# A recommendation model's interaction tower: chunk 0's shifted tiles picked by TensorE, earlier ids, products and norms, stacked context tiles

## Chip, cores and metric

The kernel runs on one core of one Trainium2 chip. The metric is the device time in microseconds of one execution. Lower is better.

## The reference

39 ids per example pick rows of 16 values from 39 tables (x, for 512 examples). Three layers then multiply fields pairwise and mix them with a weight matrix; each layer's result is divided by its norm per example, feeds the next layer, and its sum over the 16 values is a feature. Three dense layers end it.

```python
for k in range(3):
    z = jnp.einsum('bmd,bhd->bdmh', x, prev).reshape(b, D, m * h)
    t = jnp.einsum('bdc,co->bdo', z, ws[k]) + bs[k]
    t = jnp.transpose(t, (0, 2, 1))
    norm = jnp.sqrt(jnp.sum(t * t, axis=(-2, -1), keepdims=True))
    t = t / norm
    logit.append(t); prev = t
z = jnp.sum(jnp.concatenate(logit, axis=1), axis=-1)
h = jnp.concatenate([z, dense_ctx], axis=1)        # 384 + 16 features
h = jnp.maximum(h @ W_top1 + b_top1, 0.0)
h = jnp.maximum(h @ W_top2 + b_top2, 0.0)
y = h @ W_top3
```

## The kernel before

The batch is cut into 16 chunks of 32 examples. A chunk's x has 39 fields as rows and 512 columns (32 examples by 16 values).

**Gathering x.** SP loads the ids and the tables' first rows (L393, L394). POOL adds them (`make_rows`, L305) and issues ten indirect gathers for a chunk (`gather`, L320). SP stores the gathered rows to `x_scratch` in HBM (`store_chunk`, L386 to L390) and loads them back (`load_pairs`, L280, L286): three copies of x one above the other (`x_rep`, 3 x 39 rows) and, in `x_rot`, seven tiles in which the same rows stand shifted by 1, 2, ... fields. The tiles come in four groups, [0, 1], [2, 3], [4, 5], [6]; group 0's semaphore also counts x_rep. For chunk 0, ACT's queue loads groups 1 and 3.

**Layer 0.** DVE multiplies x_rep by each tile (`make_pairs`, L734), and PE sums the products with the folded w0 in seven float32 matmuls into `acc0` (`pair_matmul`, L619). `turn_x` (L607) transposes x for the scalars of the later layers.

**Layers 1 and 2.** Their products would be too many, so PE multiplies the previous result by all weights first, and ACT and DVE multiply by x afterwards. A float32 product is made of three f32r matmuls: the previous result and the weights are each split in a rounded part and the rest (`prev_hi`, `prev_lo`, `w_hi`, `w_lo`), and `three_terms` (L554 to L556) writes one PSUM bank of four fields by 128 units. A job is a layer, a chunk and a quarter of its columns; it has ten banks, D and A in turn (`PATTERN`). DVE takes the five D banks field by field (`add_field`, L756) and merges (`merge`, L775). ACT scales the five A banks (`scale_bank`, L441) and POOL adds them (`add_bank`, L333). A banks run LEAD = 7 ahead of the job that PE is in. After the merge PE turns the sum into `turned` (`turn_sums`, L595), one job later. There are 128 jobs: 0 to 3 are chunk 0 in layer 1, 4 to 7 chunk 1 in layer 1, 8 to 11 chunk 0 in layer 2, and so on in iterations of eight.

**The order around it** is written in tables of (job, place). `FINISHES` says at which A bank ACT adds the bias and squares (`finish`, L465, L468) and after which field DVE sums both (L779, L783). `NORMS` says where PE sums the squares over the units (`norms`, L632), ACT takes the root (L475), and DVE the reciprocal in four steps, the new prev (L821) and the features (L811). `HALVES_AT` says where ACT makes prev_hi (L481) and POOL prev_lo (`low`, L338). `PAIRS_AT` and `PAIR_MATMULS_AT` place the products and matmuls of layer 0 for the next chunk. Each engine works in order.

**The start.** ACT's queue loads w1, w0, the biases, w2; ACT rounds the weights (`split_high`, L424) and DVE subtracts (`split_low`, L723). PE runs `keep_busy` matmuls (L639) whose results aren't used.

**The end.** `top1` (L684) has four output tiles of four float32 matmuls: the 16 context rows (k = 0) and three features of 128 rows. Then top2 (L708) and top3 (L714).

## Time and profile before

| | us |
|---|---|
| median of 3 runs | 1101.58 (1101.01 to 1102.05) |
| the profiled execution, its own time | 1101.28 |
| its span, first to last instruction | 1099.6 |
| PE busy | 1052.5 (96%) |
| DVE busy | 969.0 (88%) |
| POOL busy | 866.9 (79%) |
| ACT busy | 780.5 (71%) |

The span is what the profiler saw between the first and the last instruction; the execution's time has 1.7 us around it. Busy shares are means over stages. The chain of waits goes back from the last instruction and says at each moment what the end hung on.

### The profile page before, as it was taken

The page shows a single profiled execution, that of the slowest core. Times are in us where ns is not written, and L with a number is a line of the kernel's source. Part 1 is how long each engine was busy: PE and PEld are TensorE (multiplying, and loading weights), DVE is VectorE, ACT ScalarE, POOL GpSimd, SP SyncE. Part 2 cuts the span into 40 slices and gives each one's busy share as a digit, 9 for nine tenths or more (in the row PEclk, how much of TensorE's full clock was granted, in tenths as well). Part 3 has the DMA queues.
Part 4 walks back from the last instruction along what each step waited for, and adds up shares of the span by engine and source line. Part 5 has one row for each costly group of instructions (what it writes and reads, how often), then busy time and mean ns, then how long its engine had stood idle before and what let it go on. Part 6 is the DMA issues. An engine that isn't in the chain of part 4 may idle for free.

```text
span 1099.6 us, 17904 instructions
## 1 busy us (share of the span) xinstructions
PE 1052.5 (96%) x4394; PEld 794.1 (72%) x4394; DVE 969.0 (88%) x3317; ACT 780.5 (71%) x2628; POOL 866.9 (79%) x726
## 2 busy tenths in 40 slices
PE   0798999999999999999999999999999999999999
PEld 0366687777778787777778777777777777788773
DVE  2467799998999999999999999999999999899892
ACT  3266586877768687776868777786868777688762
POOL 5587798888889888888888888888888888577660
PEclk9899999999999999999999999999999999999999
DMA  6503040110303011030303002030301203000000
GB/s 228 131 13 73 2 118 7 35 41 3 73 3 73 2 35 42 5 71 3 73 2 71 5 11 66 3 73 2 74 2 20 56 3 73 0 2 1 1 1 1
DMA packets 56735, 41.20 MB, mean 37 GB/s; under 512 B 37915, under 2 KB 40859, under 8 KB 56502
## 3 DMA queue, kind: packets, MB, share of 16 engines
q1 hardware_dynamic: 49145, 32.17, 12.5%
q10 hardware_dynamic: 2365, 6.60, 1.7%
q0 software_dynamic: 5120, 1.29, 1.3%
q8 instruction: 35, 0.57, 0.2%
q14 instruction: 70, 0.57, 0.2%
HBM read 38.09 MB, written 1.94 MB: 36 GB/s over the span
## 4 chain that ended last, share of the span: by engine, by line
PE 67%; POOL 21%; issue 6%; ACT 4%; DMA 1%; DVE 0%; SPq 0%; POOLq 0%; ACTq 0%
POOL sums L333 17%; PE bank_a L554 10%; PE bank_d L554 9%; PE acc L619 9%; PE bank_d L555 9%; PE bank_d L556 9%; PE bank_a L556 9%; PE bank_a L555 9%; POOL gathered L320 4%; ACT scaled L441 2%; PE turned L595 1%; ACT sums L441 1%; PE bank_a L684 1%; DMA x_pairs<-x_scratch 1%; PE bank_d L708 1%
## 5 line engine op out<-in xcount | busy, mean ns | idle before, releaser
L333 POOL TENSOR_TENSOR sums<-sums,scaled 128x512 f32<-128x512 f32 (+1 forms) x512 | 642.8, 1256 | 154.0 <-ACT scaled L441 119.3
L756 DVE SCALAR_TENSOR_TENSOR sums<-bank_d,x_col,sums 128x128 f32<-128x128 f32 x2304 | 654.8, 339 | 74.4 <-PE bank_d L556 58.8
L441 ACT ACTIVATE scaled<-bank_a,x_col 128x128 f32<-128x128 f32 x1920 | 550.6, 382 | 152.9 <-PE bank_a L556 144.4
L554 PE MATMUL bank_d<-w_hi,prev_lo 128*128 128x512 f32 x640 | 286.1, 447 | 1.2 <-DVE sums L775 0.9
L554 PE MATMUL bank_a<-w_hi,prev_lo 128*128 128x512 f32 (+1 forms) x640 | 274.5, 429 | 12.0 <-POOL prev_lo L338 6.3
L556 PE MATMUL bank_d<-w_hi,prev_hi 128*128 128x512 f32 x640 | 253.3, 396 | 0.0
L555 PE MATMUL bank_d<-w_lo,prev_hi 128*128 128x512 f32 x640 | 253.0, 395 | 0.0
L556 PE MATMUL bank_a<-w_hi,prev_hi 128*128 128x512 f32 (+1 forms) x640 | 246.2, 385 | 0.0
L555 PE MATMUL bank_a<-w_lo,prev_hi 128*128 128x512 f32 (+1 forms) x640 | 245.9, 384 | 0.0
L441 ACT ACTIVATE sums<-bank_a,x_col 128x128 f32<-128x128 f32 x512 | 146.1, 370 | 88.3 <-PE bank_a L556 88.3
L320 POOL DMA_INDIRECT gathered<-in_table,idx x160 | 177.2, 1107 | 31.9 <-issue 21.7
L554 PEld LDWEIGHTS bank_a<-w_hi,prev_lo 128*128 128x128 f32 x640 | 120.6, 188 | 66.0 <-issue 20.9
L554 PEld LDWEIGHTS bank_d<-w_hi,prev_lo 128*128 128x128 f32 x640 | 121.0, 189 | 42.0 <-DVE sums L756 8.7
L555 PEld LDWEIGHTS bank_a<-w_lo,prev_hi 128*128 128x128 f32 x640 | 121.1, 189 | 37.2 <-issue 13.7
L555 PEld LDWEIGHTS bank_d<-w_lo,prev_hi 128*128 128x128 f32 x640 | 121.7, 190 | 29.7 <-issue 10.8
L556 PEld LDWEIGHTS bank_d<-w_hi,prev_hi 128*128 128x128 f32 x640 | 121.0, 189 | 28.9
L556 PEld LDWEIGHTS bank_a<-w_hi,prev_hi 128*128 128x128 f32 x640 | 120.8, 189 | 22.7
L619 PE MATMUL acc<-z,w_sb 117*128 117x512 f32 (+1 forms) x224 | 115.9, 605 | 0.7 <-issue 0.7
L734 DVE TENSOR_TENSOR z<-x_pairs 117x1024 f32<-117x1024 f32 x64 | 106.8, 1672 | 5.1 <-DMA x_pairs<-x_scratch 4.9
L756 DVE SCALAR_TENSOR_TENSOR bank_d<-bank_d,x_col,sums 128x128 f32<-128x128 f32 x256 | 78.8, 348 | 0.0
L775 DVE TENSOR_TENSOR sums<-bank_d,sums 128x128 f32<-128x128 f32 x256 | 71.3, 279 | 0.4 <-DVE sums L756 0.4
L619 PEld LDWEIGHTS acc<-z,w_sb 117*128 117x128 f32 (+1 forms) x224 | 42.4, 195 | 15.0 <-issue 6.0
(59 smaller groups left out, 484.7 us busy)
## 6 DMA issues: line engine op xcount, KB each, us to landing
x_pairs<-x_scratch SPq DMA_DIRECT2D x141, 156.0 KB
x_pairs<-x_scratch SPq DMA_DIRECT2D x78, 78.0 KB
gathered<-in_table,idx POOLq DMA_INDIRECT x160
w_raw<-in_w ACTq DMA_DIRECT2D x2, 768.0 KB, 7.2
x_scratch<-gathered SPq DMA_DIRECT2D x16, 72.0 KB
w_raw<-in_w ACTq DMA_DIRECT2D x1, 1024.0 KB, 5.7
w_raw<-in_w ACTq DMA_DIRECT2D x1, 896.0 KB
w_raw<-in_w ACTq DMA_DIRECT2D x1, 832.0 KB
```

The lines of the kernel that those rows point to most:

```text
L320: nc.gpsimd.indirect_dma_start(out=gathered[0:n, c % 2, j, :], out_offset=None, in_=table[:, :], in_offset=bass.IndirectOffsetOnAxis(ap=id ...
L333: nc.gpsimd.tensor_tensor(out=sums[:, n % SUMS, 0:w, :], in0=sums[:, n % SUMS, 0:w, :], in1=scaled[:, a - 1, 0:w, :], op=ALU.add).then_inc ...
L441: op = nc.scalar.activation(to[:, i, :], bank_a[at % A_RING][:, i * UNITS:(i + 1) * UNITS], ACT.Copy, scale=x_of(c, q, a * PER_BANK + i))
L554: nc.tensor.matmul(to, lo, w_h, start=True, stop=False)
L555: nc.tensor.matmul(to, hi, w_l, start=False, stop=False)
L556: return nc.tensor.matmul(to, hi, w_h, start=False, stop=True)
L595: nc.tensor.transpose(turned[:, q * COLS:(q + 1) * COLS], sums[:, n % SUMS, TOTAL, :], identity[:, :]).then_inc(turn_done, 1)
L619: mm = nc.tensor.matmul(acc0[:, :], w0_sb[0:rows, tile, :], z0[0:rows, tile, :], start=(tile == 0), stop=(tile == PAIR_TILES - 1))
L684: return nc.tensor.matmul(tops[n][:, :], w[:, n * 128:(n + 1) * 128], x, start=(k == 0), stop=(k == 3))
L734: nc.vector.tensor_tensor(out=z0[0:rows, tiles[0]:tiles[0] + count, :], in0=x_rep[0:rows, :].unsqueeze(1).to_broadcast([rows, count, ROWS] ...
L756: nc.vector.scalar_tensor_tensor(out=taken(n, u) if u in LEFT else total, in0=taken(n, u), scalar=x_of(c, q, A_FIELDS + u), in1=total, op0 ...
L775: nc.vector.tensor_tensor(out=out, in0=in0, in1=in1, op=ALU.add).then_inc(merged, 1)
```

## The change

- `PICKED = 3`: tiles 0 to 2 of chunk 0's x_rot are not loaded. ACT makes nine shifted windows of the identity (`twice`, `turns`), PE multiplies x by them (`pick`) into bank_d[0] to [2], and DVE reads the products' second factor there. `pairs_landed` lets PE and DVE begin chunk 0 when x_rep is in.
- ACT's queue loads w0 and the biases first, then waits for the ids, then loads w1 and w2. POOL makes ones and identity before it waits for the ids. PE's first `keep_busy` waits for the gathers, not the store, and has five matmuls; DVE's splits wait for the gathers too.
- DVE makes prev_lo of chunk 0. It makes chunk 1's products before job 0, with w2's last three pieces between; PE's matmuls on them are in job 0.
- The norms of chunk 1 in layer 0 and of chunk 0 in layer 1 stand earlier, and the halves that follow them.
- The context's weights and values stand three times in 80 rows (0, 32, 64), rounded or rest, so that one f32r matmul gives the three terms. SP loads them six times 16 rows into cleared rows; ACT and DVE split them in job 40. `top1(0, 0..2)` is placed in the last job. `y_sb` moves into free weight space.

```diff
+PICKED = 3
...
-FINISHES = [(0, 0, None, None), (0, 1, (1, 0), (1, 5)), (1, 0, (step_at(1, 0), 3), (step_at(1, 1), 3))]
+FINISHES = [(0, 0, None, None), (0, 1, (0, 3), (0, 16)), (1, 0, (step_at(1, 0), 3), (step_at(1, 1), 0))]
...
-NORMS = [([(0, 0)], None, None, None), ([(0, 1)], (1, 6), (1, 2), (1, 12)),
-         ([(1, 0)], (step_at(1, 1), 7), (step_at(1, 1), 3), (step_at(1, 2), 2))]
+NORMS = [([(0, 0)], None, None, None), ([(0, 1)], (1, 1), (1, 0), (1, 4)),
+         ([(1, 0)], (step_at(1, 1), 3), (step_at(1, 1), 1), (step_at(1, 1), 9))]
...
-                HALVES_AT[_k + 1, _c] = (2, 0) if _k == 0 else (step_at(1, 2), 1)
+                HALVES_AT[_k + 1, _c] = (1, 3) if _k == 0 else (step_at(1, 1), 4)
...
-        _made = [(0, 1), (0, 6), (0, 11), (0, 16)]
-        _summed = {(0, 5): [0, 1], (0, 7): [2, 3], (0, 9): [4, 5], (1, 0): [6]}
+        _made = []
+        _summed = {(0, 0): [0, 1], (0, 2): [2, 3], (0, 4): [4, 5], (0, 6): [6]}
...
-        _made = [_first, (step_at(_it, 0), 12), (step_at(_it, 1), 12), (step_at(_it, 2), 5)]
+        _made = [_first, (step_at(_it, 0), 12), (step_at(_it, 1), 12 if _it > 1 else 17), (step_at(_it, 2), 5)]
...
-W2_FIRST, W2_SECOND = 3, 4
+W2_FIRST = 3
+W2_BETWEEN = {0: 3, 2: 4, 3: 5}
+CTX_ROWS = 2 * 32 + EMB
+CTX_STEP = step_at(5, 0)
+TOP_AT = {(NJ - 1, 2): 0, (NJ - 1, 4): 1, (NJ - 1, 6): 2}
...
+        twice = sb("twice", [FIELDS, 2 * FIELDS])
+        turns = sb("turns", [FIELDS, PICKED, PAIR_ROWS])
...
+        top1c_sb = sb("top1c_sb", [CTX_ROWS, TOP1], f32r)
+        ctx_sb = sb("ctx_sb", [CTX_ROWS, BATCH], f32r)
+        lows_of = sb("lows_of", [128, 2])
...
-        top1c_sb = w_raw[1][0:EMB, 12:16, :].rearrange("p a u -> p (a u)")
-        ctx_sb = w_raw[1][0:EMB, 16:20, :].rearrange("p a u -> p (a u)")
+        top1c_raw = w_raw[1][0:CTX_ROWS, 12:16, :].rearrange("p a u -> p (a u)")
+        ctx_raw = w_raw[1][0:CTX_ROWS, 16:20, :].rearrange("p a u -> p (a u)")
...
+            tiles = [i for i in PAIR_GROUPS[p] if c or i >= PICKED]
             for kk in range(PER_TILE):
...
+        def pairs_landed(c, p):
+            return 16 * ((c + 1) * PAIR_LOADS[p] - (PER_TILE if p == 0 else 0))
...
+            nc.gpsimd.memset(ones[:, :], 1.0).then_inc(ones_made, 1)
+            pool.wait_ge(ones_made, 1)
+            nc.gpsimd.affine_select(out=identity[:, :], in_=ones[:, :], pattern=[[-1, 128]], base=0,
+                                    channel_multiplier=1, compare_op=ALU.is_equal,
+                                    fill=0.0).then_inc(identity_made, 1)
             pool.wait_ge(ids_loaded, 32)
             make_rows(0)
             start_chunk(0)
             for j in range(GATHERS):
                 gather(0, j)
...
-            low(1, 0)
...
-                    sp.dma_start(top1c_sb, w_top1[3 * 128:3 * 128 + EMB, :]).then_inc(top_loaded, 16)
-                    sp.dma_start(ctx_sb, ctx_t).then_inc(top_loaded, 16)
+                    sp.wait_ge(ctx_cleared, 1)
+                    for row in range(0, CTX_ROWS, 32):
+                        sp.dma_start(top1c_raw[row:row + EMB, :],
+                                     w_top1[3 * 128:3 * 128 + EMB, :]).then_inc(top_loaded, 16)
+                        sp.dma_start(ctx_raw[row:row + EMB, :], ctx_t).then_inc(top_loaded, 16)
...
-            load_raw(1)
             act.dma_start(w0_sb[0:PAIR_ROWS, :, :], w0a).then_inc(w0_loaded, 16)
             act.dma_start(w0b_sb[0:PAIR_ROWS, :, :], w0b).then_inc(w0_loaded, 16)
             for k, b in enumerate((b0, b1, b2)):
                 act.dma_start(bias[:, k:k + 1], b).then_inc(bias_loaded, 16)
+            act.wait_ge(ids_loaded, 32)
+            load_raw(1)
             load_raw(2)
...
+            act.wait_ge(identity_made, 1)
+            nc.scalar.activation(twice[:, :].rearrange("p (k m) -> p k m", k=2),
+                                 identity[0:FIELDS, 0:FIELDS].unsqueeze(1).to_broadcast([FIELDS, 2, FIELDS]),
+                                 ACT.Copy).then_inc(twice_made, 1)
+            act.wait_ge(twice_made, 1)
+            first = twice[:, PAIR_OFFSETS[0]:]
+            assert PAIR_OFFSETS[0:PICKED * PER_TILE] == list(range(1, PICKED * PER_TILE + 1))
+            windows = bass.AP(first.tensor, first.offset, [first.ap[0], [1, PICKED * PER_TILE], [1, FIELDS]])
+            nc.scalar.activation(turns[:, :, :].rearrange("p t (k m) -> p (t k) m", m=FIELDS), windows,
+                                 ACT.Copy).then_inc(turns_made, 1)
...
+                    if (n, a) == (CTX_STEP, 1):
+                        act.wait_ge(top_loaded, TOP_LOADS * 16)
+                        nc.scalar.activation(ctx_sb[:, :], ctx_raw, ACT.Copy).then_inc(ctx_hi_made, 1)
+                    if (n, a) == (CTX_STEP, 2):
+                        nc.scalar.activation(top1c_sb[:, :], top1c_raw, ACT.Copy).then_inc(ctx_hi_made, 1)
...
-                pe.wait_ge(pairs_loaded[0], (c + 1) * PAIR_LOADS[0] * 16)
+                pe.wait_ge(pairs_loaded[0], pairs_landed(c, 0))
...
+            def pick(tile):
+                nc.tensor.matmul(bank_d[tile][0:PAIR_ROWS, :], turns[:, tile, :], x_rep[0:FIELDS, :],
+                                 start=True, stop=True).then_inc(picked, 1)
...
-                    nc.tensor.matmul(bank_d[0][:, :], ones[:, :], w_raw[1][:, 0:4, :].rearrange("p m u -> p (m u)"),
+                    nc.tensor.matmul(turned[:, :], ones[:, :], w_raw[1][:, 0:4, :].rearrange("p m u -> p (m u)"),
...
-            pe.wait_ge(scratch_stored, 48)
-            keep_busy(3)
+            pe.wait_ge(gather_done, 16 * GATHERS)
+            keep_busy(5)
+            pe.wait_ge(turns_made, 1)
+            pe.wait_ge(pairs_loaded[0], pairs_landed(0, 0))
+            for tile in range(PICKED):
+                pick(tile)
...
+                    if (n, place) in TOP_AT:
+                        pe.wait_ge(top_loaded, TOP_LOADS * 16)
+                        pe.wait_ge(ctx_made, 2)
+                        pe.wait_ge(h_ready, len(NORMS) - 2)
+                        pe.wait_ge(squared, FINISH_NO[0, CHUNKS - 1] + 1)
+                        top1(0, TOP_AT[n, place])
...
-            pe.wait_ge(top_loaded, 4 * 16)
-            pe.wait_ge(h_ready, len(NORMS) - 2)
             pe.wait_ge(a_scaled, A_BANKS * NJ)
-            pe.wait_ge(squared, FINISH_NO[0, CHUNKS - 1] + 1)
-            for n in range(2):
-                for k in range(3):
-                    top1(n, k)
+            for k in range(3):
+                top1(1, k)
...
-                dve.wait_ge(pairs_loaded[p], (c + 1) * (PAIR_LOADS[p] * 16))
+                if c == 0:
+                    dve.wait_ge(pairs_loaded[0], pairs_landed(0, 0))
+                    for i in [i for i in tiles if i < PICKED]:
+                        dve.wait_ge(picked, i + 1)
+                        mult = nc.vector.tensor_tensor(out=z0[0:PAIR_ROWS, i, :], in0=bank_d[i][0:PAIR_ROWS, :],
+                                                       in1=x_rep[0:PAIR_ROWS, :], op=ALU.mult)
+                    tiles = [i for i in tiles if i >= PICKED]
+                    if not tiles:
+                        mult.then_inc(pairs_made, 1)
+                        return
+                    count = len(tiles)
+                dve.wait_ge(pairs_loaded[p], pairs_landed(c, p))
...
+            nc.vector.memset(lows_of[:, :], 0.0).then_inc(lows_of_made, 1)
+            dve.wait_ge(lows_of_made, 1)
+            nc.vector.memset(lows_of[64:96, 0:1], -1.0).then_inc(lows_of_made, 1)
+            nc.vector.memset(lows_of[32:64, 1:2], -1.0).then_inc(lows_of_made, 1)
...
-            dve.wait_ge(ones_made, 1)
+            dve.wait_ge(gather_done, 16 * GATHERS)
             for piece in range(len(W_PIECES[1])):
                 split_low(1, piece)
-            for piece in range(W2_FIRST):
-                split_low(2, piece)
             for p in range(NP):
                 make_pairs(0, p)
-            for piece in range(W2_FIRST, W2_SECOND):
+            for piece in range(W2_FIRST):
...
+            dve.wait_ge(prev_hi_made[1], 1)
+            nc.vector.tensor_tensor(out=prev_lo[1][:, 0, :], in0=prev[:, 0, :], in1=prev_hi[1][:, 0, :].bitcast(f32),
+                                    op=ALU.subtract).then_inc(prev_lo_made[1], 1)
             features(0)
-            dve.wait_ge(prev_lo_made[1], 1)
-            for piece in range(W2_SECOND, len(W_PIECES[2])):
-                split_low(2, piece)
+            for p in range(NP):
+                if p in W2_BETWEEN:
+                    split_low(2, W2_BETWEEN[p])
+                make_pairs(1, p)
+                dve.wait_ge(w_lo_made[1], len(W_PIECES[1]))
+                nc.vector.memset(w_raw[1][0:96, 12:20, :], 0.0).then_inc(ctx_cleared, 1)
...
+                dve.wait_ge(lows_of_made, 3)
+                out, raw = ((ctx_sb, ctx_raw), (top1c_sb, top1c_raw))[at]
+                nc.vector.scalar_tensor_tensor(out=out[:, :], in0=out[:, :].bitcast(f32),
+                                               scalar=lows_of[0:CTX_ROWS, at:at + 1], in1=raw,
+                                               op0=ALU.mult, op1=ALU.add).then_inc(ctx_made, 1)
...
+                    if (n, u) == (4, 0):
+                        clear_ctx()
+                    if n == CTX_STEP and u in (12, 16):
+                        split_ctx((u - 12) // 4)
```

PE at the start (`turned`, `bank_d` and `acc` are PSUM banks, `turns` the shifted windows), before:

```order
L639 MATMUL bank_d<-w_raw,ones 128x512 [waits scratch_stored,w1_loaded0,identity_made]
L639 MATMUL bank_d<-w_raw,ones 128x512 x2
L607 MATMUL small<-identity,x_pairs 128x40 [waits pairs_loaded0]
L607 MATMUL small<-identity,x_pairs 128x40 x3
L619 MATMUL acc<-z,w_sb 128x512 [waits pairs_made,w0_folded]
L619 MATMUL acc<-z,w_sb 128x512
L619 MATMUL acc<-z,w_sb 128x512 [waits pairs_made]
L619 MATMUL acc<-z,w_sb 128x512
L619 MATMUL acc<-z,w_sb 128x512 [waits pairs_made]
```

and now:

```order
L695 MATMUL turned<-w_raw,ones 128x512 [waits gather_done,w1_loaded0,identity_made]
L695 MATMUL turned<-w_raw,ones 128x512 x4
L689 MATMUL bank_d<-x_pairs,turns 117x512 [waits pairs_loaded0,turns_made]
L689 MATMUL bank_d<-x_pairs,turns 117x512 x2
L658 MATMUL small<-identity,x_pairs 128x40 [waits pairs_loaded0]
L658 MATMUL small<-identity,x_pairs 128x40 x3
L670 MATMUL acc<-z,w_sb 128x512 [waits pairs_made,w0_folded]
L670 MATMUL acc<-z,w_sb 128x512
L670 MATMUL acc<-z,w_sb 128x512 [waits pairs_made]
```

Five matmuls stand where three stood, the first wait is for the gathers, and three picks stand ahead of the turn of x.

DVE between chunk 0's features (L811, now L884) and the first field of job 0 (L756, now L829), before:

```order
L821 TENSOR_TENSOR prev<-t,small 128x512 [waits r_step]
L811 TENSOR_TENSOR h<-small,dsum 128x32 [waits values_summed,r_step]
L723 TENSOR_TENSOR w_lo<-w_raw,w_hi 128x768 [waits w2_hi_made,prev1_lo_made]
L723 TENSOR_TENSOR w_lo<-w_raw,w_hi 128x768 [waits w2_hi_made]
L756 SCALAR_TENSOR_TENSOR sums<-bank_d,x_col,sums 128x128 [waits a_added,d_ready]
L756 SCALAR_TENSOR_TENSOR sums<-bank_d,x_col,sums 128x128 [waits a_added]
L734 TENSOR_TENSOR z<-x_pairs 117x1024 [waits pairs_summed,pairs_loaded0]
```

and now:

```order
L894 TENSOR_TENSOR prev<-t,small 128x512 [waits r_step]
L923 TENSOR_TENSOR prev_lo<-prev,prev_hi 128x512 [waits prev1_hi_made]
L884 TENSOR_TENSOR h<-small,dsum 128x32 [waits values_summed,r_step]
L785 TENSOR_TENSOR w_lo<-w_raw,w_hi 128x768 [waits w2_hi_made]
L807 TENSOR_TENSOR z<-x_pairs 117x1024 [waits pairs_summed,pairs_loaded0]
L807 TENSOR_TENSOR z<-x_pairs 117x1024 [waits pairs_loaded1]
L785 TENSOR_TENSOR w_lo<-w_raw,w_hi 128x768 [waits w2_hi_made]
L807 TENSOR_TENSOR z<-x_pairs 117x1024 [waits pairs_loaded2]
L785 TENSOR_TENSOR w_lo<-w_raw,w_hi 128x768 [waits w2_hi_made]
L807 TENSOR_TENSOR z<-x_pairs 78x512 [waits pairs_loaded3]
L829 SCALAR_TENSOR_TENSOR sums<-bank_d,x_col,sums 128x128 [waits a_added,d_ready]
```

The split of prev_lo and all four products of chunk 1 now stand ahead of the first field; one product stood behind the second field.

PE in the last job (`sums` to `turned` is the turn of a job's sum; L684, now L723, is top1), before:

```order
L554 MATMUL bank_d<-w_hi,prev_lo 128x512 [waits merged]
L555 MATMUL bank_d<-w_lo,prev_hi 128x512
L556 MATMUL bank_d<-w_hi,prev_hi 128x512
L595 MATMUL turned<-identity,sums 128x128 [waits merged]
L554 MATMUL bank_d<-w_hi,prev_lo 128x512 [waits d_added]
L555 MATMUL bank_d<-w_lo,prev_hi 128x512
L556 MATMUL bank_d<-w_hi,prev_hi 128x512
L554 MATMUL bank_d<-w_hi,prev_lo 128x512 [waits d_added]
L555 MATMUL bank_d<-w_lo,prev_hi 128x512
L556 MATMUL bank_d<-w_hi,prev_hi 128x512
L684 MATMUL acc<-w_raw 128x512 [waits a_scaled,squared,h_ready,top_loaded]
L684 MATMUL acc<-h,w_raw 128x512 x2
```

and now:

```order
L723 MATMUL acc<-ctx_sb,top1c_sb 128x512 [waits h_ready,squared,ctx_made,top_loaded]
L605 MATMUL bank_d<-w_hi,prev_lo 128x512 [waits merged]
L606 MATMUL bank_d<-w_lo,prev_hi 128x512
L607 MATMUL bank_d<-w_hi,prev_hi 128x512
L723 MATMUL acc<-h,w_raw 128x512 [waits h_ready,squared,ctx_made,top_loaded]
L646 MATMUL turned<-identity,sums 128x128 [waits merged]
L605 MATMUL bank_d<-w_hi,prev_lo 128x512 [waits d_added]
L606 MATMUL bank_d<-w_lo,prev_hi 128x512
L607 MATMUL bank_d<-w_hi,prev_hi 128x512
L723 MATMUL acc<-h,w_raw 128x512 [waits h_ready,squared,ctx_made,top_loaded]
L605 MATMUL bank_d<-w_hi,prev_lo 128x512 [waits d_added]
L606 MATMUL bank_d<-w_lo,prev_hi 128x512
```

The first three matmuls of top1 moved in between the last job's banks.

## Rows read from the trace of the kernel before

**Rows 1.** The page, part 4: shares of the chain that ended last, by engine.
```profile
PE 67%; POOL 21%; issue 6%; ACT 4%; DMA 1%; DVE 0%; SPq 0%; POOLq 0%; ACTq 0%
```
**Rows 2.** Windows, mid-run: start:end, length, busy PE, PEld, DVE, ACT, POOL, clock, DMA, GB/s.
```profile
356.00:418.00 62.00, 61.87 (x267) 47.64 (x267) 59.03 (x204) 46.93 (x161) 52.90 (x46) 1.00 0.16 34
```
**Rows 3.** Timeline of the start, POOL and SP: start us, us, engine, line.
```profile
8.68 0.48 POOL L305 TENSOR_TENSOR idx<-ids_sb,base_sb 128x10 int32<-128x10 int32 x2 [8.17 <-DMA base_sb<-in_bases]
...
20.86 0.92 POOL L320 DMA_INDIRECT gathered<-in_table,idx  x1 [0.30 <-issue]
...
23.18 0.39 SPq L386 DMA_DIRECT2D x_scratch<-gathered  x1
...
42.77 0.39 SPq L386 DMA_DIRECT2D x_scratch<-gathered  x1
```
**Rows 4.** Chain of waits, 0 to 60 us: start us, us, what.
```profile
24.25 1.94 DMA x_scratch<-gathered
...
28.23 7.15 DMA x_pairs<-x_scratch
...
36.78 8.57 PE acc L619 x14
...
50.70 1.27 POOL prev_lo L338
...
52.11 0.48 PE bank_a L554
```
**Rows 5.** DMA queue of the gathers (packets, MB, share): whole page, 13:17, 17:19.
```profile
q0 software_dynamic: 5120, 1.29, 1.3%
...
q0 software_dynamic: 62, 0.02, 1.8%
...
q0 software_dynamic: 88, 0.02, 6.2%
```
**Rows 6.** Windows of 5 us, the stream of weights.
```profile
15.00:20.00 5.00, 0.00 (x0) 0.00 (x0) 0.00 (x0) 2.86 (x4) 3.78 (x5) 1.00 0.94 364
```
**Rows 7.** Timeline, PE's warming matmuls (records, two to a matmul).
```profile
26.32 5.23 PE L639 MATMUL bank_d<-w_raw,ones 128*128 128x512 f32 x6 [26.32 <-DMA x_scratch<-gathered]
...
47.67 3.68 PE L639 MATMUL bank_d<-w_raw,ones 128*128 128x512 f32 x8
```
**Rows 8.** Timeline, DVE: the splits, and its first field of job 0.
```profile
22.04 8.61 DVE L723 TENSOR_TENSOR w_lo<-w_raw,w_hi 128x2048 fp32r<-128x2048 f32 x6 [7.30 <-POOL ones L347]
...
60.75 0.61 DVE L756 SCALAR_TENSOR_TENSOR sums<-bank_d,x_col,sums 128x128 f32<-128x128 f32 x2 [6.93 <-POOL sums L333]
```
**Rows 9.** Timeline, the first stall.
```profile
77.29 0.68 DVE L783 TENSOR_REDUCE ssq<-squares 128x32 f32<-128x512 f32 x1
...
78.02 0.41 PE L632 MATMUL small<-ssq,ones 128*128 128x32 f32 x2 [0.46 <-DVE ssq L783]
...
89.11 0.72 PE L554 MATMUL bank_a<-w_hi,prev_lo 128*128 128x512 f32 x1 [3.67 <-POOL prev_lo L338]
```
**Rows 10.** Windows of 5 us around both stalls (clock is third from the end).
```profile
85.00:90.00 5.00, 1.33 (x4) 0.76 (x4) 1.70 (x7) 0.55 (x3) 4.83 (x5) 0.92 0.03 2
90.00:95.00 5.00, 5.00 (x18) 3.91 (x17) 2.76 (x11) 2.82 (x11) 2.95 (x4) 0.74 0.21 22
...
125.00:130.00 5.00, 3.31 (x7) 2.41 (x8) 1.76 (x8) 1.47 (x6) 3.48 (x4) 0.68 0.04 3
```
**Rows 11.** Timeline, PE at the second stall and at 1037.
```profile
126.69 0.70 PE L554 MATMUL bank_a<-w_hi,prev_lo 128*128 128x512 f32 x1 [2.68 <-issue]
...
1037.39 0.50 PE L554 MATMUL bank_a<-w_hi,prev_lo 128*128 128x512 f32 x1 [1.87 <-POOL prev_lo L338]
```
**Rows 12.** Timeline, PE in the last job.
```profile
1070.39 0.50 PE L554 MATMUL bank_d<-w_hi,prev_lo 128*128 128x512 f32 x1 [0.92 <-DVE sums L775]
```
**Rows 13.** Chain of waits, the end.
```profile
1079.21 2.96 PE bank_a L684 x6
...
1088.71 6.87 PE bank_d L708 x16
```

33 lines of the change are left out of this document (19 added, 14 removed).

## Prediction

> **What bounds the kernel now.** I read the page first. Its chain that ended last is 67% PE and 21% POOL [rows 1]. The windows then tell which part is which: in one of the middle iterations of eight jobs, 62.00 us, PE is busy 61.87 us, DVE 59.03 and POOL 52.90 [rows 2]. So the middle is bound by the matmuls, which the change leaves alone. It can only win where PE waits: ahead of the first job, at two stalls in the first dozen jobs, and after the last bank.
>
> The timeline of the start shows the order of the waits. POOL's first gather has to wait for the ids, which land at 8.68; the tenth gather is issued at 20.86 and its data is in at 23.18, when SP stores the rows; chunk 1's gathers are in at 42.77 [rows 3]. The chain continues with the store (landed at 26.19), the loads of the shifted x (landed at 35.38), 14 records of pair matmuls (8.57 us), the first norm, POOL's prev_lo (1.27 us), and the first bank at 52.11 [rows 4]. A float32 matmul is two records here.
>
> **Part 1, the start.** Ids: SP issues them at the same moment as before, but the 5.1 MB of weights now wait for them, and only w0 (0.8 MB) runs beside them. The store's landing after its last issue, 1.94 us [rows 4], is the nearest row of a short transfer in peace; that bounds them at 3.6 from below, 8.68 bounds from above. I take 5.2, a gain of 3.5. The ten gathers keep their 12.2 us (8.68 to 20.86, [rows 3]), so the last is issued at 17.4 and leaves POOL at 18.4. Identity and ones now come ahead, in time in which POOL waited anyway.
>
> Not all of that arrives. The gathers' queue needs 5120 packets for 160 gathers, 32 each; under the weight stream it moved 62 packets in 13 to 17 us and 88 in 17 to 19 [rows 5]. So at 19 it had served fewer than five gathers of the eight issued. From POOL's end of the last one (21.78) to SP's store passed 1.4 us. The weights now start after the ids, near 6.5, and at 364 GB/s, the rate of 15 to 20 [rows 6], their 5.1 MB last 14 us, to 20.5: all ten gathers run under the stream. I take 20.7 for their end (18.4, the old 1.4, and 0.9 of backlog, which is 38 packets at the 44 a microsecond of 17 to 19), between 19.8 (no backlog) and 23.2 (all gain lost). The Trainium skill, "DMA: Bandwidth & Descriptors", section "Latency and other measured facts", gives 0.2 us of HBM latency on average and 2 us at high load; by it the last gather lands up to 1.8 us later than in peace, near 21.6. No row here shows a latency by itself, so the sum doesn't use it.
>
> Store and x: the store takes 3.0 us as before (23.18 to 26.19), to 23.7. Before, PE waited for group 0 among chunk 0's 23 blocks of 39 rows, 9.2 us from 26.19 to 35.38 [rows 4]. Now it waits for the three copies of x alone, SP's first three transfers, and chunk 0 has 14 blocks. With ACT's queue loading beside them, six to seven blocks go by until they are in: 0.3 of 9.2 is 2.8, and with 0.8 for the issues it makes 3.6: x_rep at 27.3.
>
> PE: keep_busy(5) is ten records from 20.7. At the pace of the first six (5.23 us) they take 8.7 us, at that of the later eight (3.68 us) 4.6 [rows 7]; the middle, 6.7, ends just as x_rep lands. The three picks are six records at the fast pace, 2.6 us; with the turn of x the pair matmuls begin at 30.6. They are 14 records; since PE has not paused they take 14 x 0.43 = 6.0 us (0.43 is the step of the 16 records of [rows 13]), not 8.57. DVE's share hides: it splits w1 in three of the six pieces of 8.61 us (5.7 us, [rows 8]: 4992 of 7680 columns) from 20.7 on, done at 26.4, before the first pick; and its products, near the 0.68 us that it takes for 128x512 in [rows 9], stay ahead of PE's 0.86 per tile. Pairs end at 36.6 instead of 45.35.
>
> From there to the first bank stays, 6.76 us, less 0.6 for prev_lo on DVE (0.68 again) instead of POOL's 1.27 [rows 4]: 42.8 against 52.11. **Term 1: -9.3 us**, with ends of -5.5 (gathers at 23.2, pairs at 8.57) and -11.5 (ids at 3.6, no backlog). By the skill's loaded latency it would be -8.4.
>
> **Part 2, chunk 1's products ahead of the jobs.** Worth nothing by itself. DVE sat idle 6.93 us up to 60.75, waiting for POOL's sums [rows 8], and PE does the same seven matmuls, which bound job 0. The price is the cover: DVE may begin job 0 only when chunk 1's loads have landed. Its gathers were in 19.6 us after chunk 0's (23.18 to 42.77, [rows 3]); identity no longer stands between, 1.3 us, so 39.0. Store 3.2 and loads some 10 (an estimate from chunk 0's 9.2 to group 0) end at 52; with a last split and product DVE begins at 54. PE's D0 comes at 42.8 + 6.84 = 49.7; it needs DVE to have emptied that bank for D3, 9.6 us on, at 59. Slack of four us: zero.
>
> **Part 3, the earlier norms.** First stall: before, PE waited 0.46 us for the squares of chunk 1 and 3.67 us for its prev_lo [rows 9]; the windows show what followed, clock 0.92 over 85 to 90 and 0.74 over 90 to 95: (0.08 + 0.26) x 5 = 1.7 us of work lost [rows 10]. Together 5.8. Now PE asks for the norm at place 1 of job 1: 11 banks of 0.70 (three records of 0.232, from 267 in 61.87), one of 0.53, seven pair matmuls of 0.86 and a turn of 0.37, with 0.3 for changes of type, put that 14.9 us after D0. The squares are later: A10 ends at 11.8, ACT scales it (1.1) and writes t (0.7) by 13.9, DVE sums (0.7), does three fields and two merges (1.2) and squares (0.7): 16.5. So PE waits 1.6 us instead of 0.46. prev_lo is then ready at 26.6 (POOL: bank 14's sum at 22.9, two gathers of 1.2, 1.27), ahead of its use at 27.6, unless a gather is held. After the wait of 1.87 us at 1037 the clock fell, after that of 0.92 at 1070 it didn't [rows 11, 12]; I charge half of 1.7, and 0.4 for prev_lo: 1.6 + 0.9 + 0.4 = 2.9. **-2.9**, ends 0 and -4.5.
>
> Second stall: 2.68 us [rows 11], clock 0.68 over 125 to 130 [rows 10], 1.6 more: 4.3. The half is made two A banks earlier and its norm four places earlier, 3 us ahead of need. At its norm PE may wait 0.3; chunk 2's products may come late since its gathers do not move, 0.3. 2.68 + 1.6 - 0.6 = 3.7: **-3.7**, ends -1 and -4.3. The wait at 1037 stays.
>
> **Part 4, the end.** Top1 is four groups of three matmuls, the context one first. A group takes 2.96 us [rows 13]: six records of 0.43 (the step of top2's 16) are 2.58, and 0.38 goes into the change between 16 and 128 rows. Stacked over 80 rows in f32r the context matmul is one record of 0.23; banks of 512 and 384 columns show that a matmul's time goes by its columns. With half of the 0.38 left a group is 0.23 + 1.72 + 0.2 = 2.2, so four groups save 3.0. The first now lies in the last job, where PE waits 0.92 us for DVE at 1070.39 [rows 12] and two short times more, 1.1 in all, which it fills. DVE's last merge comes 0.4 later for it and PE may wait 0.3 at turn_sums or at the last squares. 3.0 + 1.1 - 0.3: **-3.8**, ends -2.5 and -4.8. ACT's two copies, DVE's two splits (0.7 each) and the clear lie in jobs where both have room: +0.3.
>
> Sum: -9.3 - 2.9 - 3.7 - 3.8 + 0.3 = -19.4. The profiled execution took 1101.28 (span 1099.6); it gives 1081.9; the median of the three runs, 1101.58, stands 0.3 above it: **1082.2**. Likeliest case with its unknowns: 1078.5 to 1085.
>
> **Rivals.**
> - *The gathers starve.* For: the 62 packets in four microseconds of [rows 5]. Against: 44 a microsecond in 17 to 19, more than the 26 that POOL issues (32 per 1.22 us). If the gathers end at 23 and PE runs the pairs at half pace, the start gains 5 to 6: 1085.5.
> - *New stalls with a slow clock.* The norm at place 1 waits 2 us and POOL's two gathers hold prev_lo again; part 3 gives 1 to 3 instead of 6.5: 1086.
> - *Everything tighter.* Ids at 4, stalls gone: 1077.
> - *The gain doesn't carry.* POOL's work per job in the first iteration (four sums of 1.27, three gathers of 1.22, 8.7 us) is above PE's 7.75 of 62 for eight; if POOL holds the ring over the first ten jobs, that is up to 1 us a job, and part 3's gain goes too, 6.5: 1098 at worst, 1094 in the middle.
> - *Slower.* DVE may not touch job 0 before chunk 1's x is there. Were those loads to land past 59, each microsecond is one of PE's; only past 79 does it eat the 20. Before, with later gathers, they were in time for a product behind the second field at 60.75, so it takes a queue that is stuck: 1104.
>
> **Chances.** Forecast 0.55, starved gathers 0.14, new stalls 0.14, tighter 0.11, not carried 0.04, slower 0.02. 0.2% is about what a measurement can tell here. Faster 0.97, same 0.01, slower 0.02. The range 1076.5 to 1088 takes in all but the last two and the edges.
>
> **What would show it.** First bank near 42.8, gathers' end near 20.7, pair records 0.43 apart; one wait under 2 us on the squares of chunk 1 and none on prev_lo before 1000; the 61.9 in 62 unchanged; no float32 record at 16 rows, and top2's first record some 8.1 us after the last turn_sums (9.6 before). It is wrong if the first bank is past 47, if a wait on prev_lo remains near job 4, or if the middle changes.

## The result, and the profile after

| | before | forecast | after |
|---|---|---|---|
| median, us | 1101.39 (6 runs) | 1082.2 (1076.5 to 1088.0) | 1092.24 (1090.27 to 1092.48, 6 runs) |
| ratio to before | | | 0.9912 (95%: 0.99 to 0.9925) |
| span of the profiled execution | 1099.6 | | 1090.4 |

The change is faster by 9.2 us, or 0.9%, less than half of what was forecast, and the range missed it. The middle of the run is as before [rows 2]. Page of the change, busy times, and the window of the same iteration:

```profile
PE 1050.6 (96%) x4400; PEld 793.4 (73%) x4400; DVE 972.2 (89%) x3326; ACT 784.2 (72%) x2632; POOL 864.9 (79%) x725
```

```profile
356.00:418.00 62.00, 61.83 (x267) 47.63 (x266) 58.97 (x205) 47.83 (x163) 53.07 (x44) 1.00 0.16 34
```

Landmarks show where the 9.2 us came from (a turn is the transpose of a job's sum, `turn_sums`; the last column says what the stretch up to this line gained or lost):

| us | before | forecast | after | after - before | of it in this stretch |
|---|---|---|---|---|---|
| first bank | 52.11 | 42.8 | 48.70 | -3.4 | -3.4 |
| turn of job 3 | 103.80 | | 99.61 | -4.2 | -0.8 |
| turn of job 4 | 114.18 | | 113.03 | -1.1 | +3.0 |
| turn of job 6 | 135.89 | | 130.43 | -5.5 | -4.3 |
| turn of job 124 | 1059.16 | | 1053.94 | -5.2 | +0.2 |
| end of the span | 1099.6 | | 1090.4 | -9.2 | -4.0 |

Timeline of the start, POOL and SP, which answers to [rows 3]:

```profile
5.21 0.49 POOL L338 TENSOR_TENSOR idx<-ids_sb,base_sb 128x10 int32<-128x10 int32 x2 [3.83 <-DMA base_sb<-in_bases]
...
17.32 0.92 POOL L353 DMA_INDIRECT gathered<-in_table,idx  x1 [0.30 <-issue]
21.77 2.31 POOL L338 TENSOR_TENSOR idx<-ids_sb,base_sb 128x10 int32<-128x10 int32 x1 [3.52 <-DMA gathered<-in_table,idx]
24.24 2.29 POOL L353 DMA_INDIRECT gathered<-in_table,idx  x1 [0.17 <-DMA x_scratch<-gathered]
...
36.88 3.30 POOL L353 DMA_INDIRECT gathered<-in_table,idx  x1 [0.30 <-issue]
```

```profile
21.71 0.39 SPq L418 DMA_DIRECT2D x_scratch<-gathered  x1
...
42.77 0.39 SPq L418 DMA_DIRECT2D x_scratch<-gathered  x1
```

The ids are there at 5.2, as forecast. But the last gather, issued at 17.3, is in at 21.7, and POOL waits 3.52 us for it. When POOL had issued all ten, at 18.24, their queue had moved only 211 of their 320 packets; before, at the same point (21.78), it had moved 288. The queue in the windows 0:18.24 and 18.24:22:

```profile
q0 software_dynamic: 211, 0.06, 1.4%
...
q0 software_dynamic: 109, 0.02, 3.0%
```

Chunk 1's gathers are in at 42.77, to the hundredth when they were in before. There, the first of them was issued 2.1 us later, but it and the nine others were through sooner; POOL's timeline before:

```profile
26.34 2.21 POOL L320 DMA_INDIRECT gathered<-in_table,idx  x1 [0.17 <-issue]
28.84 1.62 POOL L320 DMA_INDIRECT gathered<-in_table,idx  x1 [0.30 <-issue]
...
35.76 1.69 POOL L320 DMA_INDIRECT gathered<-in_table,idx  x1 [0.30 <-issue]
...
40.29 1.15 POOL L320 DMA_INDIRECT gathered<-in_table,idx  x1 [0.30 <-issue]
```

Timeline of PE in the same stretch ([rows 4, 7]), and the windows (clock is third from the end):

```profile
21.83 6.31 PE L695 MATMUL turned<-w_raw,ones 128*128 128x512 f32 x10 [21.83 <-DMA gathered<-in_table,idx]
30.00 3.23 PE L689 MATMUL bank_d<-x_pairs,turns 39*117 39x512 f32 x6 [1.86 <-DMA x_pairs<-x_scratch]
...
33.55 9.00 PE L670 MATMUL acc<-z,w_sb 117*128 117x512 f32 x14
```

```profile
30.00:35.00 5.00, 5.00 (x12) 2.42 (x13) 3.05 (x5) 0.30 (x1) 3.78 (x5) 0.72 0.25 52
35.00:40.00 5.00, 5.00 (x8) 2.04 (x7) 4.36 (x5) 0.00 (x0) 4.70 (x2) 0.59 0.03 3
```

PE finishes its warming at 28.1 and pauses 1.86 us for x_rep. In the picks and the pair matmuls behind it the granted clock is at the lower of its two levels (1.2 of 2.4 GHz) for a part of the time, 0.72 over 30 to 35 and 0.59 over 35 to 40: 14 records take 9.0 us, where 6.0 were forecast. DVE up to its first field of job 0 (before at 60.75, [rows 8]):

```profile
52.57 1.73 DVE L807 TENSOR_TENSOR z<-x_pairs 117x1024 f32<-117x1024 f32 x1 [3.04 <-DMA x_pairs<-x_scratch]
...
62.29 1.76 DVE L807 TENSOR_TENSOR z<-x_pairs 78x512 f32<-78x512 f32 x1
63.98 4.21 DVE L829 SCALAR_TENSOR_TENSOR sums<-bank_d,x_col,sums 128x128 f32<-128x128 f32 x16
```

And every wait of PE over 1 us behind the start, which answer to [rows 9, 11]:

```profile
72.23 0.41 PE L683 MATMUL small<-ssq,ones 128*128 128x32 f32 x2 [1.51 <-DVE ssq L856]
...
84.51 0.50 PE L605 MATMUL bank_a<-w_hi,prev_lo 128*128 128x512 f32 x1 [1.45 <-POOL prev_lo L371]
...
91.37 0.50 PE L605 MATMUL bank_d<-w_hi,prev_lo 128*128 128x512 f32 x1 [1.70 <-DVE sums L848]
...
102.36 1.10 PE L670 MATMUL acc<-z,w_sb 117*128 117x512 f32 x2 [2.48 <-DVE z L807]
...
1032.13 0.63 PE L605 MATMUL bank_a<-w_hi,prev_lo 128*128 128x512 f32 x1 [1.88 <-POOL prev_lo L371]
```

Two of these, 1.70 and 2.48 us, did not exist before. The one at 126.69 [rows 11] is gone, and so is the slow clock around it. Chain of the end, against [rows 13]:

```profile
1071.25 0.33 PE turned L646
...
1079.54 6.87 PE bank_d L770 x16
```

### The profile page after: what moved, and what is told of

Read it like the earlier page. It is cut to its first block, busy times and chain, and to the rows that moved or that the text cites. A ratio compares the mean times of both kernels' runs of the same rounds, so it can differ in the third digit from the quotient of the medians.

```text
span 1090.4 us, 17939 instructions
## 1 busy us (share of the span) xinstructions
PE 1050.6 (96%) x4400; PEld 793.4 (73%) x4400; DVE 972.2 (89%) x3326; ACT 784.2 (72%) x2632; POOL 864.9 (79%) x725
## 4 chain that ended last, share of the span: by engine, by line
PE 67%; POOL 21%; issue 4%; ACT 3%; DVE 2%; DMA 2%; SPq 1%; POOLq 0%; DVEq 0%; ACTq 0%
POOL sums L366 16%; PE bank_a L605 9%; PE bank_d L605 9%; PE acc L670 9%; PE bank_d L606 9%; PE bank_d L607 9%; PE bank_a L607 9%; PE bank_a L606 9%; POOL gathered L353 4%; ACT scaled L476 1%; ACT sums L476 1%; PE turned L646 1%; DMA x_pairs<-x_scratch 1%; PE bank_d L770 1%; DMA gathered<-in_table,idx 1%
## 5 line engine op out<-in xcount | busy, mean ns | idle before, releaser
L829 DVE SCALAR_TENSOR_TENSOR sums<-bank_d,x_col,sums 128x128 f32<-128x128 f32 x2304 | 653.4, 337 | 63.6 <-PE bank_d L607 51.5
L605 PEld LDWEIGHTS bank_a<-w_hi,prev_lo 128*128 128x128 f32 x640 | 120.4, 188 | 60.8 <-issue 17.2
L807 DVE TENSOR_TENSOR z<-x_pairs 117x1024 f32<-117x1024 f32 (+2 forms) x63 | 103.3, 1643 | 6.2 <-DMA x_pairs<-x_scratch 6.2
L829 DVE SCALAR_TENSOR_TENSOR bank_d<-bank_d,x_col,sums 128x128 f32<-128x128 f32 x256 | 78.7, 346 | 0.0
```

The costliest lines, as they stand in the source:

```text
L605: nc.tensor.matmul(to, lo, w_h, start=True, stop=False)
L807: nc.vector.tensor_tensor(out=z0[0:rows, tiles[0]:tiles[0] + count, :], in0=x_rep[0:rows, :].unsqueeze(1).to_broadcast([rows, count, ROWS] ...
L829: nc.vector.scalar_tensor_tensor(out=taken(n, u) if u in LEFT else total, in0=taken(n, u), scalar=x_of(c, q, A_FIELDS + u), in1=total, op0 ...
```

## The experiments

Theory A: the start fell short because PE's clock fell. Theory B: the x of chunks 1 and 2 comes too late for an earlier start. All ratios are to the kernel before on the same chip; e, f and r are labels. The change itself has two ratios, 0.9912 (the result above) and 0.9894 (r0), and each run is held against both. "Both edits" means e5.

**The start's pause (e1).**

```diff
-            keep_busy(5)
+            keep_busy(7)
```

> The changed kernel with seven warming products instead of five ahead of the picks. Its own time is 1092.2 us. Theory A (the start was lost to the clock): TensorE no longer idles the 1.86 us before x_rep lands at 29.9, the 14 pair records run at the full clock and the first bank starts at 45.7 instead of 48.7; if this is carried to the end the time is 1089.3. Theory B (the x of chunks 1 and 2 arrives too late for an earlier start): the first bank is at 45.7 too, but TensorE then waits longer for products of chunk 1, whose x lands at 52.6 as before, and of chunk 2; the time is 1091 to 1092.2.

1096.38 us, ratio 0.9942 (0.9927 to 0.9958): slower than the change, and slower than either theory had it. The first bank was earlier by 1.1 us (47.6), and the turn of job 1 came at 82.23 against 82.10. PE's timeline shows where the 1.1 us went, and what came later:

```profile
65.57 0.47 PE L605 MATMUL bank_d<-w_hi,prev_lo 128*128 128x512 f32 x1 [0.97 <-DVE sums L829]
...
104.58 2.04 PE L670 MATMUL acc<-z,w_sb 117*128 117x512 f32 x2 [4.65 <-DVE z L807]
```

PE runs into a bank that DVE hasn't emptied, and waits 0.97 us. The 4.65 us at 104.58 is chunk 2's x: its store was issued as in the change (91.10), its loads only at 95.96 instead of 93.98. Over 100 to 110 the clock was 0.66; the change's profile kept it at 1.00 there. The pair records took 8.0 us although PE had not paused, so the clock can fall there without a pause.

**Chunk 2's gathers (e2).** `GATHERS_BEFORE = 6` instead of 3.

> The changed kernel with six of chunk 2's ten gathers ahead of the jobs instead of three, in the 5.3 us in which GpSimd idles before its first add at 51.9. Theory B (the wait of 2.48 us at 102.4 for chunk 2's products, and the 1.45 and 1.70 us behind GpSimd at 84.5 and 91.4, come of the gathers inside jobs 0 to 2): the last gather is issued some 10 us earlier than 88.7, the 2.48 us go, and of the other 3.15 us some; the time is 1087 to 1089.7. Theory A (these waits are not the gathers' doing, or something else is late next): 1092.2, less than 1 us off. [...]

1085.50 us, 0.9852 (0.9838 to 0.9866): 4 to 7 us below the change, somewhat more than theory B had. SP stores chunk 2 at 78.97, not 90.97, and in the table of PE's waits the prev_lo of chunk 1, the merge and chunk 2's products are gone; what is left of prev_lo is the one near 1025:

```profile
78.97 0.38 SPq L418 DMA_DIRECT2D x_scratch<-gathered  x1
```

```profile
PE bank_a L605 <- POOL prev_lo L371: 1.9, 1, 1.9
...
PE acc L670 <- DVE z L807: 0.6, 2, 0.5
```

**Chunk 1's gathers (e3).** Besides this edit, `idx` gets a third row.

```diff
-        gather_done = sem("gather_done")
+        gather_done = [sem(f"gather{i}_done") for i in range(2)]
...
-                if c >= 1:
-                    pool.wait_ge(gather_done, c * 16 * GATHERS)
+                if c >= 2:
+                    pool.wait_ge(gather_done[c % 2], (c // 2) * 16 * GATHERS)
```

> The changed kernel with one count of landed gathers for the even chunks and one for the odd, and a third row of indices, so that GpSimd doesn't wait from 18.2 to 21.8 for chunk 0's gathers before it issues chunk 1's. Theory B: chunk 1's gathers land at 33 to 39 instead of 42.8, its products are made before job 0's adds, VectorE begins these before 64.0 by several us, and the time falls by 0.5 to 2 us, to 1090.2 to 1091.7. Theory A (chunk 1's x is not what bounds): within 0.5 us of 1092.2. A rival: the gathers share the DMA queues with chunk 0's stores and loads, x_rep lands 1 us or more after 29.9, and the time is 1093.

1089.51 us (1084.19 to 1091.71), 0.9894 (0.9877 to 0.9911): by time alone it can't be told from the change. The profiled execution is the fastest of the four. In it chunk 1 is stored at 34.23, and DVE begins job 0 at 56.41 instead of 63.98. This profile had the full clock through the start and the first bank at 45.60; the turn of job 0 came at 72.08, 3.1 us before the change's, so here an early start was carried. POOL's stop of 2.28 us before a gather is gone too, and with it PE's wait on prev_lo.

**The second stall alone, on the kernel before (e4).** The change's four table entries for chunk 0 in layer 1 (finish, norm, halves, and `12 if _it > 1 else 17` for chunk 2's third product) and nothing else.

> The kernel before with only the second early norm of the change: that of layer 1, chunk 0, with its finish, halves and the shifted products of chunk 2. It prices the stall at 126.7. By my forecast this part is worth 3.7 us (ends 1 and 4.3): 1097.7. By the trace of the change, in which the stretch from the turn at 113 to the one at 130.4 is 4.3 us shorter: 1097.1. By the rival, a new wait takes most of it: 1100.4.

1098.79 us, 0.9972 (0.9963 to 0.9981): 3.1 us by the ratio, 3.65 by the medians, and 3.9 in the traces (from the turn of job 3 to that of job 6, 28.2 us instead of 32.1). The rival of 1100.4 us is out.

**The change again (r0)**, as the measure for the three below.

> The changed kernel itself, on the chip of the runs beside it, as the measure for them: 9 to 10 us below the kernel before.

1089.71 us, 0.9894 (0.9879 to 0.991). This profile shows both theories at work. PE:

```profile
28.85 2.80 PE L689 MATMUL bank_d<-x_pairs,turns 39*117 39x512 f32 x6 [0.39 <-DMA x_pairs<-x_scratch]
...
31.81 6.28 PE L670 MATMUL acc<-z,w_sb 117*128 117x512 f32 x14
...
44.24 0.48 PE L605 MATMUL bank_a<-w_hi,prev_lo 128*128 128x512 f32 x1
...
53.98 1.96 PE L670 MATMUL acc<-z,w_sb 117*128 117x512 f32 x4 [1.80 <-DVE z L807]
```

The clock held, the pairs took 6.28 us, and the first bank stood at 44.24, 4.5 us ahead of the other profile of the same kernel. But PE then waited 1.80 us for chunk 1's products, and the turn of job 0 (72.75) was 2.4 us ahead. Then came 2.70 us for chunk 2's products and, over 100 to 105, a clock of 0.66; at the turn of job 4 (112.14) r0 was 0.9 us ahead. Of 4.5 us, 3.6 were lost.

**Both edits (e5)**: e2 and e3 together.

> The changed kernel with both edits: separate counts for even and odd chunks' gathers, and six of chunk 2's gathers ahead of the jobs. If the two act on different waits (the counts let VectorE begin job 0 early, so that an earlier first bank is carried; the six gathers take chunk 2's products out of TensorE's way) the gains add: 7 us from the gathers and 1 to 3 from the counts, 1082 to 1084.5. If they act on the same wait it stays at the 1085.5 of the six gathers alone.

1080.82 us, 0.9823 (0.9805 to 0.9841), a little below the 1082 to 1084.5 of gains that add. Since the medians mix executions with and without a fall of the clock, the clearest comparison is between those whose mean granted clock was 1.000:

| clock 1.000 throughout | change (r0) | e3 | e2 | e5 |
|---|---|---|---|---|
| us | 1087.44 | 1084.19 | 1084.57 | 1078.43, 1080.54, 1080.82 |

Alone the two edits give 3.2 and 2.9 us, together 6.6 to 9.0: the gains add, though the first three numbers are of one execution each. First bank 45.91, turn of job 0 at 72.37, and no wait of PE over 1.1 us between the start's and the one at 1022 but that for the squares (1.50).

**Longer warming (e6, e8)**, both edits and

```diff
-            pe.wait_ge(gather_done[0], 16 * GATHERS)
-            keep_busy(5)
+            keep_busy(17)
```

(21 in e8).

> The same two edits, and TensorE's warming begins when the first weights are in (near 12 us) with 17 matmuls, which end near 30, instead of five from the gathers' end at 21.7. Theory A (the clock fell at 32 to 39 because TensorE paused 1.9 us and had run only 6 us): the clock stays at 1.00 through the picks and the 14 pair records, which take 6.3 us instead of 8.0 to 9.0; with VectorE free the 2 to 3 us are carried to the end: 1080 to 1082. If the clock falls there whatever TensorE did before: no difference to both edits without it.

> Both edits (separate counts, six gathers) with 21 warming matmuls from the first weights (10.6 us); at the 0.96 us of each that the run with 17 shows they end near 30.8, when x_rep lands (30.5). The run with 17 ended at 27.0, paused 3.5 us and ran picks and pairs at clock 0.50 to 0.58. If the pause ahead of the picks is what lets the clock fall, it stays at 1.00 now, the first bank is at 46.2 and the time is 1080.5 to 1082, with less spread than both edits alone (1078.4 to 1083.3). If the clock falls there also without a pause, as a part of it did with seven matmuls from 21.9, the time is 1083 or more.

e6: 1084.66 us, 0.9854 (0.984 to 0.9867), slower than e5. The 34 records of warming took 16.41 us, 0.48 each, and so ended at 27.0 and not near 30; PE paused 3.54 us, and picks and pairs ran at the low clock. Its timeline and window:

```profile
30.52 5.15 PE L689 MATMUL bank_d<-x_pairs,turns 39*117 39x512 f32 x6 [3.54 <-DMA x_pairs<-x_scratch]
```

```profile
35.00:40.00 5.00, 5.00 (x10) 2.29 (x9) 4.23 (x6) 0.30 (x1) 4.09 (x4) 0.50 0.32 30
```

e8: 1082.96 us (1081.33 to 1089.33), 0.9839 (0.9815 to 0.9863), no gain over e5. Without a pause the clock stayed at 1.00, the pairs took 6.28 us, and the first bank stood where e5's did. The expected smaller spread didn't come: in the profile the clock fell elsewhere (0.94 over 1012 to 1043), and the execution of 1089.33 us, which has no profile, had a mean clock of 0.995.

**Part 2 and the first early norm undone (e7)**: the tables of chunk 1 as before, `make_pairs(1, p)` ahead of job 0 removed.

> The changed kernel with chunk 1's products and pair matmuls back inside job 0, and its finish, norm and halves back at their old places; the early norm of layer 1 stays. Theory B says that VectorE, free at 52, begins job 0 some us earlier than 64.0, but that the first stall (0.5 and 3.7 us, with a slow clock behind it) comes back: 1093 to 1096. By the prediction's part 3 the loss is 2.9 us, 1095.1. If part 2 was itself a cost above what the early norm gives, the time is below 1092.2.

1088.35 us, 0.9881 (0.9866 to 0.9896), against r0's 0.9894: no loss that can be measured, where 1093 to 1096 was expected. The stall of 3.71 us came back, the waits of 1.50, 1.35, 1.70 and 2.70 went or shrank. The turn of job 0 came at 72.96 behind a first bank at 48.50; in the change it came at 75.18 behind one at 48.70. So up to that turn this half costs about 2 us: two records (0.86 us) that it moved from job 1 into job 0, and the wait of 1.5 us for the squares, which stands ahead of that turn. It comes back behind it, where the stall of 3.71 us is gone. By time, this half of the change is worth nothing that these runs can measure.

**The weights' stream (e9)**: `load_raw(2)` behind x_rep.

> A look at the start only: the changed kernel with w2 (2.5 of the 5.1 MB of weights) issued after chunk 0's x_rep has landed. If the stream of weights is what holds the last gather for 3.5 us (issued by 18.2, in at 21.7) and the loads for 4 to 5 us, the gathers are in at 19.7 and x_rep at 26.5 to 27.5. If not, both stay at 21.7 and 28.9 to 29.9. The time as a whole says little, since w2's splits now stand in ACT's and VectorE's way: 1090 to 1096.

The last gather, issued at 17.77, was in at 20.17, 1.5 us after it left POOL instead of 3.5. But x_rep still took 5.4 us from the store's landing (23.1 to 28.5), so in this one execution (1089.23 us) the stream held the gathers and not the loads. When POOL had issued all ten, 288 of the 320 packets had been moved, as before the change. Chunk 1's gathers were in at 38.97, 3.8 us earlier than in the change, and the early start was carried: first bank at 43.89, turn of job 0 at 70.67, which is 4.8 and 4.5 us ahead of the change's profile.

**The norm at place 3 (e10)**: both edits, `(1, 3)` for `(1, 1)`.

> Both edits, and the norm of chunk 1 in layer 0 asked for at place 3 of job 1 instead of place 1. TensorE waited 1.5 us there for VectorE's squares in every run with the change; two banks (1.4 us) now stand ahead of it and nothing that hangs on the norm comes later, as it couldn't start before. 1.4 us below both edits alone: 1079.4. If the banks only run into VectorE's ring of banks instead, no difference: 1080.8.

The wait of 1.50 us is gone and the turn of job 6 is 1.1 us earlier (120.33 against 121.47), but the time, 1082.41 us, 0.9828 (0.9815 to 0.984), isn't. None of its five executions kept a mean clock of 1.000, three of e5's did; the profile lost it behind the wait at 1020. At 0.997, where both have executions, e10 took 1081.90 to 1082.48 and e5 1083.14 and 1083.25: 1 us for the edit.

**The end (e11)**: `TOP_AT = {}`, the first three of top1 behind the last bank.

> The changed kernel with the first three matmuls of top1 back behind the last bank; the stacked context stays. By the prediction's part 4 the overlap fills 1.1 us of waits and costs 0.3: 0.8 us slower than the change, and stacking is the rest of the 3.8. If the overlap is what gives most, 2 us slower.

1092.34 us, 0.9917 (0.9902 to 0.9933). The spread hides the 0.8 us that was expected. In the traces it is, from the turn of job 124 to the end of the span 36.8 us, against 36.5 in the change and 40.4 before. The overlap is worth 0.3, the stacking and the rest 3.6, by one profile each.

**Beyond the change (f1, f2)**: e10, and for chunk 15 the norm of layer 1 earlier as the change does it for chunk 0; f2 with `GATHERS_BEFORE = 10`.

```diff
+    if _it == CHUNKS - 1:
+        NORMS.append((_items, (step_at(_it, 5), 3), (step_at(_it, 5), 1), (step_at(_it, 5), 9)))
+        continue
```

> Separate counts, six gathers and the norm at place 3 as in e10, and the norm of chunk 15 in layer 1 with its finish and halves 4 places or more earlier, as the change does for chunk 0. TensorE waits 1.88 us there in every run, and behind it the clock of the window 1012 to 1043 was 0.94 in five profiles of nine, which is 1.9 us of work. The wait gone: 1.9 us less; the fall of the clock behind it gone too: 1 us more on average and a smaller spread. 1079 to 1080 against e10's 1082.4. If something else is late there at once: 1082.

> f1 with all ten of chunk 2's gathers ahead of the jobs, in the 8.9 us that GpSimd idles before its first add. The first adds come at 48.8 and the gathers end near 47, so nothing is held there; the four gathers that leave jobs 0 and 1 free GpSimd 4.9 us, but no engine waited for it there with six: no difference to f1, within 1 us. [...]

f1: 1081.01 us, 0.9813 (0.98 to 0.9826), and all five runs lie within 1.0 us, where e10's lay within 3.3 (counted over all profiles, the clock had fallen behind that wait in 11 of 15, not in five of nine). At a mean clock of 0.997 f1 is 1.1 us below e10; by the ratios the two aren't told apart. f2: 1077.97 us, 0.9792 (0.9776 to 0.9808), the fastest of all, 11 to 14 us below the change. The gathers gave none of its 3 us over f1: from the turn of job 0 (74.55 in f1, 70.95 in f2) to the one at 1043.42 and 1039.79 both keep their distance. It is the start again; f1's PE:

```profile
30.54 3.72 PE L693 MATMUL bank_d<-x_pairs,turns 39*117 39x512 f32 x6 [2.41 <-DMA x_pairs<-x_scratch]
...
34.57 8.51 PE L674 MATMUL acc<-z,w_sb 117*128 117x512 f32 x14
```

**The ids' share (f3)**: the change with w1's loads ahead of w0 and of the ids.

> The changed kernel with w1's three loads issued at once, as before the change, ahead of w0 and with no wait for the ids; w2 follows. The ids then land near 8.7 instead of 5.1, all gathers move by 3.5 us, and so do chunk 1's and chunk 2's, since they follow on GpSimd: 3.5 us slower than the change (1089.7 to 1092.2), 1093.2 to 1095.7. If the later jobs absorb it, since they wait for other things, 1 us slower.

1093.27 us (1089.71 to 1094.09), 0.9918 (0.9905 to 0.9931), so 1 to 3 us slower than the change (0.9894 and 0.9912), with intervals that overlap the latter's. The ids were in at 8.50, 3.3 us later than in the change, the gathers at 23.4, only 1.7 us later: under the stream of weights half of the ids' gain was lost before SP stored a row.

## Why the prediction missed

Forecast were 19.4 us in the profiled execution, 9.2 came. By the landmarks the 10.2 between them are: the start 5.9; the first stall 2.1; the stretch to the turn of job 4, where chunk 2's products came late, 3.0; and less 0.6 for the second stall and 0.3 for the middle and the end. The forecast's own signs of being wrong were both there, a first bank past 47 and a wait on prev_lo near job 4.

**What bounds, and part 4: right.** The middle kept its time. The end gave 4.0 us for 3.8, and the context's work in the middle cost 0.2 for 0.3. Inside the end the two shares were off, and that they cancelled was luck: the overlap gave 0.3, not 0.8, and the stacking 3.6, not 3.0.

**Part 3, second stall: right in size.** 4.3 us in the change's trace, 3.1 to 3.9 alone (e4), against 3.7.

**Term 1, the start: three steps mis-sized.** Of the 5.9 us between 42.8 and 48.70: the gathers' end came 1.0 late (21.7). The Trainium skill, "DMA: Bandwidth & Descriptors", section "Latency and other measured facts", gives 2 us of HBM latency at high load, and by it the prediction had 21.6. The trace has 21.7, but that the number agrees is luck: no latency of the last gather is seen in it. The queue was behind by 77 packets besides those of the last gather (211 of 320 moved at 18.24), where the sum had a backlog of 38; with w2 out of the stream (e9) it was not behind, and the last gather landed 1.5 us after it had left POOL. "3.6 us from the store's landing to x_rep" was 5.2 (4.2 to 5.7 over the profiles), 1.6 late; the proportion of blocks, 6 or 7 of 23, doesn't hold, and the stream isn't the reason, since e9 took 5.4. What is stays open. And "ends just as x_rep lands", on which the full clock rested, failed by 1.86 us: picks and pairs took 12.6 us from x_rep for 9.3, 3.3 late. That is theory A, and it holds for some executions only (r0 took 9.2). That the clock fell is shown; that the pause made it fall is not (last section). Two readings inside the sum are off without weight: w1's splits are 5.6 us by their own proportion (5.51 measured), not 5.7, and D0 came 7.07 us behind the first bank, not 6.84. From the last pair to the bank it took 6.14 us, as forecast.

**Part 2, the slack of four us: wrong.** I had "identity no longer stands between" move chunk 1's gathers to 39.0, and counted "a last split and product" of DVE as two us. POOL waited 3.5 us for chunk 0's gathers to land, the sum of the ids took 2.31 us, and then, starting 2.1 us earlier than before, chunk 1's ten gathers took 17.2 us (24.24 to 41.41) instead of 15.1 (26.34 to 41.44), held beside DVE's splits and products. So chunk 1 was in at 42.77, the same hundredth as before by chance. From the first of its products to the last took 11.4 us (52.57 to 63.98), since four products and two splits, beside POOL, lie there; DVE began job 0 at 64.0, not 54. In this trace that cost nothing by a wait of PE, since the first bank was late too. But a first bank at 42.8 would have helped by half at most: r0, at 44.24, lost 2.1 of its 4.5 us at the first turn, e2 waited 1.48, e1 0.97; e3, e5 and e9, in which chunk 1's gathers were in by 34 to 39, carried theirs.

**Part 3, first stall: mis-sized.** 2.9 us forecast, 0.8 came. The 1.6 us for the squares were right (1.51). What the forecast set aside with "unless a gather is held" is what happened: POOL stood 2.28 us before a gather at 82.20, prev_lo came 1.45 late, DVE's merge behind POOL 1.70. The trace of the kernel before had shown it: there POOL stood 2.09 us before the gather at 84.18, on the chain that led to the 3.67 us on prev_lo. So it belonged in the sum and not in an "unless".

```profile
84.18 0.96 POOL L320 DMA_INDIRECT gathered<-in_table,idx  x1 [2.09 <-issue]
```

Chunk 2's gathers, which hang on the same engine, ended at 89.6 for products that PE wants at 99.9: 2.48 us and the +3.0 of the table. The prediction had put 0.3 on it. e2, which only issues three of these gathers earlier, removes all three waits and gains 4 to 7 us by the ratios (2.9 between executions whose clock never fell), more than any other single edit to the change.

**The rivals.** Three came in part, and together. "The gathers starve": they did, but ended at 21.7 and not at 23. "New stalls": PE waited 1.51 us for the squares, a gather held prev_lo again (this time without a slow clock), and part 3 gave 0.8 and 4.3 less the 3.0, 2.1 in all, inside this rival's 1 to 3. "The gain doesn't carry", which had 0.04: it didn't, but for the late x of chunks 1 and 2 and not for POOL's sums. Each was priced alone (1085.5, 1086, 1094); what they cost adds.
